# Cross-attention stage of a transformer kernel: projections of a row in the odd half, turns of queries and keys in the next even half

## The reference

```python
x = x + _L1_xattn_ref(_layernorm(x), ctx_2048, ...)   # 16 heads of 16, queries and keys normalised (rms) before the scores
...
q = rms_norm(x @ Wq + bq, gq); k = rms_norm(ctx @ Wk + bk, gk); v = ctx @ Wv + bv
scores = jnp.einsum('bqnd,bknd->bnqk', q, k) * scale
probs = jax.nn.softmax(scores, axis=-1)
out = jnp.einsum('bnqk,bknd->bqnd', probs, v) @ Wo + bo
...
x = x + _L1_ffn_ref(_layernorm(x), ...)               # 256 -> 1024 -> 256, activations and weights rounded to 4 bits
```

## Time and profile before

| | us |
|---|---|
| median of 3 timed runs | 1276.08 |
| lowest, highest | 1270.59, 1281.32 |
| profiled execution, its own time | 1287.0 |
| its span, from the first to the last instruction | 1285.2 |
| mean granted clock of TensorE | 0.952 |
| stage s23, steps of windows 0 to 15 on TensorE | 429 to 547 |

### The profile page before, as it was taken

The page is one execution under the profiler, slowest core; times in us unless marked ns, Lnnn a source line. Parts: engine busy times, 40 slices in busy tenths (PEclk is TensorE's granted clock), DMA queues, the critical chain, the costliest instruction groups (busy, mean ns, idle before and its releaser), DMA issues.

```text
span 1285.2 us, 20553 instructions
## 1 busy us (share of the span) xinstructions
PE 1089.5 (85%) x7122; PEld 824.9 (64%) x7138; DVE 705.3 (55%) x1700; ACT 506.4 (39%) x1789; POOL 320.5 (25%) x440
## 2 busy tenths in 40 slices
PE   1788886999996788799999999996788999985684
PEld 0355543899995466588888888884555666653463
DVE  5777755212223778854555445555656666664334
ACT  0155562223231466643334333332445555542121
POOL 5543310222222354420000000002122222210562
PEclk9999996899998798999999999998989999998797
DMA  6443205898882070000000000140000000000785
GB/s 186 126 132 109 84 31 186 321 327 327 330 321 88 1 263 2 1 28 20 1 2 1 1 1 1 33 132 1 1 1 9 5 5 5 6 5 11 239 258 175
DMA packets 59731, 121.31 MB, mean 94 GB/s; under 512 B 9049, under 2 KB 37481, under 8 KB 53713
## 3 DMA queue, kind: packets, MB, share of 16 engines
q1 hardware_dynamic: 52217, 106.62, 25.0%
q0 software_dynamic: 4416, 12.06, 2.8%
q10 hardware_dynamic: 2996, 1.32, 0.4%
HBM read 107.29 MB, written 12.49 MB: 93 GB/s over the span
## 4 chain that ended last, share of the span: by engine, by line
PE 61%; DVE 17%; issue 7%; ACT 6%; DMA 4%; POOL 2%; SPq 1%; ACTq 0%; another core or an unknown queue 0%; DVEq 0%; POOLq 0%
PE P L865 6%; PE P L875 6%; PE P L1788 4%; PE P L1781 4%; PE P L1833 4%; PE P L1797 4%; DVE small L468 3%; ACT big L2185 3%; PE P L2705 2%; PE P L1926 2%; PE P L1806 2%; PE P L1821 2%; PE P L1932 2%; PE P L329 1%; PE P L1977 1%
## 5 line engine op out<-in xcount | busy, mean ns | idle before, releaser
L139 POOL TENSOR_TENSOR lrs<-lve,mhalf 128x1 f32<-128x1 f32 x64 | 36.7, 574 | 365.2 <-DVE lve L130 333.1
L468 DVE TENSOR_REDUCE small<-P 128x2 f32<-128x512 f32 x128 | 83.4, 681 | 40.4 <-PE P L293 39.5
L2096 ACT ACTIVATE big<-P,small 128x128 f32<-128x128 f32 x128 | 45.4, 367 | 145.0 <-DVE small L2274 145.0
L905 ACT ACTIVATE big<-P,big 128x128 f32<-128x128 f32 x184 | 52.6, 369 | 122.5 <-PE P L865 105.3
L544 ACT ACTIVATE big<-P 128x512 f32<-128x512 f32 x128 | 72.0, 598 | 60.0 <-PE P L311 54.2
L865 PE MATMUL P<-big 128*128 128x128 f32 x736 | 87.4, 278 | 0.8 <-DMA big<-b_w 0.7
L865 PEld LDWEIGHTS P<-big 128*128 128x128 f32 x736 | 85.2, 194 | 1.9 <-DMA big<-b_w 1.3
L875 PE MATMUL P<-big 128*128 128x256 f32 x368 | 83.1, 379 | 0.0
L293 PE MATMUL P<-big 90*128 90x256 bf16 x256 | 55.5, 306 | 31.8 <-DMA big<-scr_qk 17.2
L2265 DVE COPY big<-P 128x512 f32<-128x512 f32 x32 | 22.1, 692 | 107.0 <-PE P L1797 107.0
L998 DVE COPY big<-P 128x256 f32<-128x256 f32 x23 | 9.8, 425 | 126.0 <-PE P L875 126.0
(11 more groups left out here) (386 smaller groups left out, 2582.2 us busy)
## 6 DMA issues: line engine op xcount, KB each, us to landing
big<-b_w SPq DMA_DIRECT2D x23, 1028.0 KB
big<-b_w SPq DMA_DIRECT2D x23, 1024.0 KB
big<-scr_qk SPq DMA_DIRECT2D x96, 96.0 KB
big<-i_wgu SPq DMA_DIRECT2D x23, 352.0 KB
big<-moe_y SPq DMA_DIRECT2D x16, 256.0 KB, 4.2
big<-i_wd SPq DMA_DIRECT2D x23, 176.0 KB
scr_qk<-big SPq DMA_DIRECT2D x8, 384.0 KB
moe_x<-XN SPq DMA_DIRECT2D x16, 128.0 KB, 1.7
```

Source lines behind the costliest of these rows:

```text
L468: dve.tensor_reduce(negM[:, h, :], P[:, h % 2, :].rearrange("p (c s) -> p c s", c=2), AX.X, ALU.max, negate=True).then_inc(a_max, 1)
```

## The change

For rows 2 to 7, projections and turns change places, and all engines follow:

- TensorE: `project_context`, `project_rows` and the new `project_values` of row k + 2 are done in the odd half of row k, in this order (they were in the even one); `turn` of row k + 1 is done in its preceding even half, that of row k (it was in the odd half of row k - 1). The values have a function and a semaphore (`c_vj`) of their own, and wait for the copy of the rows turned in the same half (`tb_ev`, `TURNED[n - 2]`, for a row n = k + 2; before, all projections waited for those of a row earlier, `TURNED[n - 3]`), since they share bank 1 with `turn_rows`.
- VectorE: `copy_probs` comes right behind `maxima`; `normalise` stands in the even half behind it, `bias` and `values` in the odd half, ahead of its second `divide`.
- ScalarE: `copy_qk` in the even half, `squares` in the odd half behind `copy_rows`.
- GpSimd: `diagonal` is cut into its two instructions, of which one stands before and one behind the reciprocal root of the feed-forward part in the even half; `rms` comes last in the odd half.
- `weigh` of an odd half waits for `divide` of the half before by a wait of its own (`c_o`).

Rows 0 and 1 keep their places.

```diff
@@ TensorE
-                if n >= 4:
-                    pe.wait_ge(tb_ev, TURNED[n - 3])
-                for w, dst in ((1, P[:, QK_BANK[n], D:2 * D]), (2, P[:, V_BANK[n], 0:D])):
-                    for k in range(KD):
-                        pe.matmul(dst, CT[:, k, n * T:n * T + T], cw[:, k, w * D:w * D + D], start=(k == 0),
+                for k in range(KD):
+                    pe.matmul(P[:, QK_BANK[n], D:2 * D], CT[:, k, n * T:n * T + T], cw[:, k, D:2 * D], start=(k == 0),
+                              stop=(k == KD - 1))
+
+            def project_values(n):
+                if n >= 3:
+                    pe.wait_ge(tb_ev, TURNED[n - 2])
+                for k in range(KD):
+                    t = pe.matmul(P[:, V_BANK[n], 0:D], CT[:, k, n * T:n * T + T], cw[:, k, 2 * D:3 * D], start=(k == 0),
                                   stop=(k == KD - 1))
+                t.then_inc(c_vj, 1)
...
-                if c == 0 and n > 0:
+                if c == 1:
+                    pe.wait_ge(c_o, h)
+                elif n > 0:
                     pe.wait_ge(c_x, n)
...
                 if bank == 1:
-                    pe.wait_ge(c_v, min(k + 3, B))
+                    pe.wait_ge(c_v, min(k + 2, B))
...
-                    if 2 <= k + 2 < B:
-                        project_context(k + 2)
-                        project_rows(k + 2)
+                    if 2 <= k + 1 < B:
+                        turn(k + 1)
                     elif k == -2:
                         project_rows(0)
                 else:
                     if 0 <= k - 1 < B:
                         turn_rows(k, 1)
-                    if 0 <= k + 2 < B:
+                    if 2 <= k + 2 < B:
+                        project_context(k + 2)
+                        project_rows(k + 2)
+                        project_values(k + 2)
+                    elif k + 2 in (0, 1):
                         turn(k + 2)
@@ ScalarE
-                    if 0 <= k + 2 < B:
+                    if k + 2 in (0, 1):
                         squares(k + 2)
+                    if 2 <= k + 1 < B:
+                        copy_qk(k + 1)
                 else:
                     if 0 <= k - 1 < B:
                         copy_rows(k, 1)
-                    if 0 <= k + 2 < B:
+                    if k + 2 in (0, 1):
                         copy_qk(k + 2)
+                    elif 2 <= k + 2 < B:
+                        squares(k + 2)
@@ VectorE
             def values(n):
+                dve.wait_ge(c_vj, n + 1)
...
@@ GpSimd
+                    if 2 <= k + 1 < B:
+                        diagonal(k + 1, 0)
                     if 0 <= k - 3 < B:
                         ln_rsqrt(pool, LN_FIRST + 2 * B + LN23["feed", k - 3], LN23["feed", k - 3] % 2)
-                    if 0 <= k + 2 < B:
+                    if 2 <= k + 1 < B:
+                        diagonal(k + 1, 1)
```

More of the change, by code:

```diff
@@ L1116, in build @@
             sem("c_" + n) for n in ("ld pj tr s t pv y qkf v qkn mx PTv rz o x ss qkT exp PT cb ve rs kbd").split())
+        c_vj = sem("c_vj")
         HALVES = 2 * B
@@ L1332, in s23_pe @@
             pe.wait_ge(c_ld, 112)
-            project_context(0)
-            project_context(1)
+            for n in range(2):
+                project_context(n)
+                project_values(n)
             turn_routed(0)
@@ L1538, in s23_dve @@
                     maxima(w + 1)
-                if odd and 0 <= k + 2 < B:
+                if 0 <= w < HALVES:
+                    copy_probs(w)
+                if odd and k + 2 in (0, 1):
                     normalise(k + 2)
+                if not odd and 2 <= k + 1 < B:
+                    normalise(k + 1)
                 if odd and 0 <= w - 1 < HALVES:
                     divide(w - 1)
-                if 0 <= w < HALVES:
-                    copy_probs(w)
                 if not odd:
@@ L1559, in s23_dve @@
                         quantise(k - 2, 0)
+                    if 2 <= k + 2 < B:
+                        bias(k + 2)
+                        values(k + 2)
                     if 0 <= w < HALVES:
@@ L1576, in rms, with diagonal @@
                 pool.tensor_tensor(c_rst[:, n % 2, :], c_vet[:, n % 2, :], mhalf[:, 0:2], ALU.pow).then_inc(c_rs, 1)
-            def diagonal(n):
+            def diagonal(n, c):
                 pool.wait_ge(c_qkT, n + 1)
-                for c in range(KD):
-                    if n >= 2:
-                        pool.wait_ge(c_s, 2 * n - 3 + c)
-                    pool.tensor_tensor(c_kb[n % 2][:, c], c_qT[n % 2][:, 2 + c:3 + c, :].broadcast_to([128, 4, T]),
-                                       hm.rearrange("p (j a) -> p j a", a=1).broadcast_to([128, 4, T]),
-                                       ALU.mult).then_inc(c_kbd, 1)
+                if n >= 2:
+                    pool.wait_ge(c_s, 2 * n - 3 + c)
+                pool.tensor_tensor(c_kb[n % 2][:, c], c_qT[n % 2][:, 2 + c:3 + c, :].broadcast_to([128, 4, T]),
+                                   hm.rearrange("p (j a) -> p j a", a=1).broadcast_to([128, 4, T]),
+                                   ALU.mult).then_inc(c_kbd, 1)
             def bias(n):
@@ L1631, in s23_pool @@
                         bias(k)
-                    if 0 <= k + 2 < B:
-                        diagonal(k + 2)
+                    if k + 2 in (0, 1):
+                        for c in range(KD):
+                            diagonal(k + 2, c)
                     if 0 <= k - 1 < B:
                         quantise(k - 1)
+                    if 2 <= k + 2 < B:
+                        rms(k + 2)
             for what in (("attend", B - 1), ("feed", B - 3)):
```

## The result

The changed kernel is a little slower: 1.0044 times the kernel before, 95% interval 1.0028 to 1.0061, 13 runs each. That ratio is +5.6 us of 1277; the medians, 1283.49 against 1277.13 us, differ by 6.4. The two kernels compared again on another occasion gave 1.0025 (1.0009 to 1.0040), which is +3.2 us. The profiled execution has a span of 1285.4 us, where the one before had 1285.2; that these agree is an accident of the last stage, and is taken up behind the table of runs.

What follows compares the result with a forecast made beforehand. Each row was taken as bound by a loop from odd-half weigh through VectorE's whole queue to the probabilities' copy and the next weigh. Terms +2.8, +0.7, +0.4 and -1 gave +2.9 on 1276.1: 1279 us, range 1270 to 1288.

Steps and rivals of the forecast that it cites:

- What goes: Odd half: TensorE's waits at turn and weigh lose their cause; squares and rms are free; normalise falls to 0.8 us.
- The even half: Projections (2.59 us) leave, turn comes; turn waits about 1.1 us, up 1.1 more; the half is as long as before.
- term 4: TensorE's clock: as many slow stretches as before, waits 3.9 us a row for 2.8, some 1 us less loss seen: -1.
- The odd half and the loop: Values' projection waits for ScalarE's copy_rows behind eight exponentials; new loop from weigh to weigh, 15.4 us, 16.3 with port hindrance.
- term 1: Full rows, halves 6 to 11: three rows of 16.3 us against 15.38, +2.8 us.
- The bounded term: VectorE's feed-part apply beside GpSimd's second diagonal: hindrance between nothing and 0.9 us, taken as 0.9.
- Rival D: Old and new loop come out alike, 15.4 us each, no port hindrance, filling's gain used up: 1276 us; chance 0.22.
- The last halves: Last two halves before the stage drains: 13.7 us against 13.0, +0.7 us.
- Filling: Halves 0 to 5: -1.8 and -0.7 in the first two, +2.0 and +0.9 after, together +0.4 us.
- the first three terms: Order of steps in the stage: full rows +2.8, last two halves +0.7, filling +0.4 us.
- B: VectorE becomes the bound, values wait for nothing, a row takes 14.5 us; -5 us, 1271 in all; chance 0.22.
- C: TensorE waits in three places, clock falls in every row at 2.7 us each, 16 on top: 1295 us; chance 0.08.

Runs made afterwards that it cites:

- a_rows: Changed kernel with ScalarE's copy_rows moved ahead of the exponentials in the odd half; 0.9996 of the kernel before.
- a_pair: Changed kernel with GpSimd's second diagonal after the feed part's apply, and weigh ahead of up in the even half; 0.9998 of the kernel before.
- a_diag: Changed kernel with GpSimd's second diagonal waiting until VectorE's apply of the feed part is through; 1.0015 of the kernel before.
- a_both: Changed kernel with copy_rows ahead of the exponentials and the second diagonal after the apply; 0.9989 of the kernel before.
- filled versions: Changed kernel and kernel before, each with twelve added identity transposes a row on TensorE; 1.0008 and 0.9996 of the kernel before.
- r_after: Changed kernel run again, unedited, against the kernel before on the same chip; 1.0025 of the kernel before.
- a_fill: Changed kernel with six identity transposes before turn and six before up in each even half on TensorE; 1.0008 of the kernel before.
- a_weigh: Changed kernel with weigh ahead of up on TensorE in the even half, nothing else; 1.0003 of the kernel before.
- r_before: Kernel before run again, unedited, for a second profile; 1.0000 of the kernel before.
- b_fill: Kernel before with twelve identity transposes ahead of each turn of rows 2 to 7 on TensorE; 0.9996 of the kernel before.

## Why the prediction was right or wrong

The measured time (1283.5, +5.6 us by the ratio) lies in the range, on the side forecast, and within 1% as given the highest chance. The size was 2.9. That the second comparison gave +3.2, close to it, is in part luck: two parts of the sum were off in opposite directions, the order (3.9 for 2.7) and the clock (-1 for a loss).

- **What goes**: as written. weigh's wait for the copy is gone in full rows, rms and squares cost nothing, normalise fell to 0.87 us.
- **The even half**: right. turn waits 0.90 (forecast 1.1), up 1.04 (1.1). With the 1.14 of the values the waits of a row come to 3.1 us, where term 4 had 3.9.
- **The odd half and the loop**: the wait at the values is 1.14 us and a_rows shows that this loop sets the row. Its length was forecast at 16.3 and is 16.0. The three full rows, cleaned of the clock, cost +2.0 us where term 1 had +2.8.
- **The bounded term**: the apply takes 1.13 us beside the diagonal and 0.41 without, so the hindrance is real, but it is 0.7 us (0.5 in the start of the maxima: 1.05 us behind the apply's, against 0.55 in a_pair) and not the 0.9 that I took; the prediction's own rows, 1.12 and 0.41, gave 0.7. And the step "the loop is then 16.3, without it 15.4" was wrong. Without it the row is still 16.0 (a_diag), since the path through scores and ScalarE's copy is as long. I had followed VectorE's queue alone to the exponentials, and had not put ScalarE's copy_probs, which stands ahead of them, into the sum. As to the rule of the Trainium skill ("SBUF — State Buffer", "SBUF: two separate sides"): 1.13 and 1.12 us beside a diagonal, 0.41 without, agree with it, and yet its price in the time of the row was nothing in the changed kernel (0.2 us once the copies of rows are out of the way, a_rows against a_both). Rival D's "15.4 each" falls with the same step.
- **The last halves**: +0.65 us without the clock, forecast +0.7. **Filling**: forecast +0.4, 43.3 against 43.9 us in the filled versions, one of which has a low stretch there. The order alone thus costs 2.7 us in halves 6 to 13, where the first three terms had 3.9.
- **The clock**: this is the term that was mis-sized, in its sign too. I took "as many such stretches as before" and -1 us, since "some 1 us less of their loss is seen". In the profiles it is +2.6 us in halves 6 to 13, and up to 0.8 more in the filling. In halves 6 to 13 the low stretches of the changed kernel begin in the even half, at up or weigh behind two waits of about 1 us. Weigh and scores stand there on one of the two paths that set the row, so 1.5 to 1.6 us of each such row are lost for good; I had reckoned that longer waits elsewhere would hide them. With 2.7 for the order, 2.6 for the clock and 0.8 that can't be divided, the sum is the stage's 6.1, and near the upper of the two timed differences (5.6). The lower one (3.2) has little room for a clock term, and so has the mean clock of the timed runs (0.951 against 0.950). So the loss in the profiled executions is shown; how large it is in the mean of many executions stays open.
- **Rivals**: B (the change does what the waits suggest) needed the values to be free, and a_rows with this one step mended gives 14.98 us and 0.9996, so it was one queue position away, but not the 14.5 us that I gave it. C named the right mechanism at a fraction of its strength: in halves 6 to 13 three rows of four were hit in each profile of the changed kernel, not each, and for 1.6 us, not 2.7. The sign that the prediction gave for C, a granted clock under 0.9 in most slices from 450 to 545 us, did appear in the first profile (0.89, 0.95 and 0.89 from 449.8, 482 and 514 us on), though the time was not C's; in r_after one of the three slices was under 0.9, as in the first profile of before.

## What to carry to other kernels

When a step is moved out of one wait, follow each engine's whole queue to the place where it lands, and walk all paths that end there, not the busiest one: here eight exponentials stood between a transposition and the bank that the moved projection needed, and two paths of the same length hid the gain of either being shortened. Several waits of one microsecond on TensorE can cost more than their sum when the clock falls behind them; work for two of the waits (a_fill), or the third wait ahead of scores instead of up (a_weigh), gave back 2 to 5 us of the 1280 here by the ratios, the lower end of which is inside the noise, with the rows as long as before. The length of a row in the trace, at full clock, tells edits apart that ten timed runs of the whole kernel can't; but one profile of a stage does not say how often the clock falls.

## What the hardware showed that I had not expected

- With waits of 0.90, 1.04 and 1.14 us, spread over a row of 16.0 us in which TensorE was busy for 12.9, the granted clock fell to 1.2 GHz in some rows and not in others, four times in the 122 us of the stage (one of them in the filling, behind a longer wait). Twelve transposes a row, in two of the three waits, went with a granted clock of 1.00 from 440.75 us to the end of the stage in a_fill. But so did a_weigh hold it without any work added, with waits of 0.90, 0.71 and 1.38 us in a row, 3.0 together against 3.1 in the changed kernel. So the idle time of a row alone does not say whether the clock falls, and that it was the cause in the changed kernel is not shown; why this arrangement holds the clock and the other doesn't stays open.
- A stretch at 1.2 GHz does not cost the same everywhere: 1.5 to 1.6 us of a full row in the changed order, 1.2 to 1.5 in the order before, 0.3 to 0.4 in the last weigh but one of the order before (scores to the last weigh 10.95 us in r_before and 11.02 in b_fill, 10.64 without it).
- The last stage differed by 11 us (94.0 and 105.2) between executions of one kernel on different occasions, with DMA rates of 231 and 206 GB/s, so about the same bytes. What made the rate differ no run here shows.
